# A shared feed-forward stage and an expert stage joined into one program: weights split early, experts unrolled, two scatters in flight

## The reference

```python
x = x + attention0(layernorm(x), ctx, ctx)
# mixture of experts, E = 8, top 2, I = 352, shared part SI = 704
f = layernorm(x); scores = softmax(f @ gate_w.T)
w = scores * one_hot(top_k(scores, 2)).sum(1)
g, u = split(einsum('nh,eih->nei', f, experts_gate_up))
out = einsum('neh,ne->nh', einsum('nei,ehi->neh', silu(g) * u, experts_down), w)
shared = silu(f @ shared_gate_w.T) * (f @ shared_up_w.T) @ shared_down_w.T
x = x + out + sigmoid(f @ shared_expert_gate_w.T) * shared
x = x + attention1(layernorm(x), ctx, ctx)
x = x + low_rank_experts(layernorm(x))    # gates by the first token
```

## Time and profile before

| what | us |
|---|---|
| median of 3 runs | 612.63 (612.49 to 616.44) |
| the profiled execution | 613.12 |
| span of its trace, first to last instruction | 611.3 |
| mean granted TensorE clock | 0.927 |
| PE / DVE / POOL / ACT busy | 489.3 / 296.7 / 213.2 / 194.1 |
| shared stage's last matmul ends | 252.7 |
| expert matmuls begin / end | 256.0 / 416.7 |
| attention 1 begins | 460.5 |

### The profile page before, as it was taken

One profiled execution on the slowest core, in us unless ns is written; L12 is line 12 of the kernel. 1 busy time (PEld: TensorE's weight loads), 2 busy tenths in 40 slices (PEclk: granted clock), 3 DMA queues, 4 the chain that ended last, 5 costly groups with the idle time before them and its releaser, 6 DMA issues. The chain is left out here.

```text
span 611.3 us, 9853 instructions
## 1 busy us (share of the span) xinstructions
PE 489.3 (80%) x3126; PEld 393.3 (64%) x3127; DVE 296.7 (49%) x674; ACT 194.1 (32%) x426; POOL 213.2 (35%) x259
## 2 busy tenths in 40 slices
PE   4799996599999998748999999992004798998587
PEld 3567663476877775647999999991003566666465
DVE  4678785631541211224455554441006478977574
ACT  2455543474500210012333333330002355453044
POOL 3110320343403773342793222233224436420055
PEclk9999999699999998879999999997556899999799
DMA  8993000200001325259412222211107200000003
GB/s 306 395 387 99 1 1 0 80 0 2 1 0 38 109 92 122 71 201 358 165 34 72 80 71 69 69 55 41 43 34 254 90 1 1 1 2 2 0 19 120
DMA packets 37747, 53.30 MB, mean 87 GB/s; under 512 B 8945, under 2 KB 31986, under 8 KB 37458
## 3 DMA queue, kind: packets, MB, share of 16 engines
q1 hardware_dynamic: 28482, 23.19, 12.9%
q0 software_dynamic: 6032, 22.55, 10.2%
q10 hardware_dynamic: 3200, 7.14, 3.2%
HBM read 35.78 MB, written 17.10 MB: 86 GB/s over the span
## 5 line engine op out<-in xcount | busy, mean ns | idle before, releaser
L112 POOL TENSOR_TENSOR rstd<-var,mhalf 128x2 f32<-128x2 f32 x32 | 22.6, 706 | 137.2 <-DVE var L105 137.2
L1174 PE MATMUL banks<-w_hi,xgT_hi 128*128 x156 | 57.1, 367 | 11.1 <-POOL w_lo L1143 7.7
L1252 ACT ACTIVATE hg<-banks 128x352 f32<-128x352 f32 x39 | 18.1, 465 | 123.2 <-PE banks L1178 123.2
L1310 DVE TENSOR_TENSOR hgT_lo<-banks,hgT_hi 128x256 fp32r<-128x256 f32 x78 | 24.1, 351 | 67.4 <-ACT hgT_hi L1260 67.4
L411 DVE TENSOR_REDUCE mx<-banks 128x16 f32<-128x1024 f32 x32 | 39.1, 1223 | 32.2 <-PE banks L272 31.8
L1175 PE MATMUL banks<-w_lo,xgT_hi 128*128 x156 | 51.5, 331 | 0.0
L272 PE MATMUL banks<-kvb,qT 64*128 64x256 f32 x256 | 36.3, 401 | 17.8 <-ACT qT L358 6.6
L944 PE MATMUL banks<-sdn,big 128*128 128x256 f32 x192 | 49.0, 403 | 0.0
L148 PE MATMUL banks<-ctxT,wk 128*128 128x128 f32 x16 | 4.1, 439 | 51.3 <-PEq L1112 43.8
L944 PEld LDWEIGHTS banks<-sdn,big 128*128 128x128 f32 x192 | 35.1, 195 | 13.2 <-issue 9.3
L123 ACT ACTIVATE xn<-x,shift,rstd 128x256 f32<-128x256 f32 (+1 forms) x64 | 34.7, 593 | 27.5 <-POOL shift L114 26.3
(11 more groups left out here) (223 smaller groups left out, 1162.2 us busy)
## 6 DMA issues: line engine op xcount, KB each, us to landing
w_hi<-in_egu POOLq DMA_DIRECT2D x2, 2816.0 KB, 21.3
expert_rows_in<-zeros SPq DMA_DIRECT2D x1, 5304.0 KB, 42.2
xn<-expert_rows_in SPq DMA_DIRECT2D x39, 128.0 KB, 2.1
w_lo<-in_egu ACTq DMA_DIRECT2D x3, 1408.0 KB, 9.9
y_all<-choices_out SPq DMA_DIRECT2D x16, 256.0 KB, 5.9
out_x<-fo SPq DMA_DIRECT2D x8, 256.0 KB, 2.1
x<-in_x ACTq DMA_DIRECT2D x2, 768.0 KB, 11.3
d_hi<-in_edown POOLq DMA_DIRECT2D x1, 1536.0 KB, 7.8
```

The source lines that it names most:

```text
L112: nc.gpsimd.tensor_tensor(m["rstd"][:, b, :], m["var"][:, b, :], m["mhalf"][:, :], ALU.pow).then_inc(self.rstd_ready, 1)
L1174: nc.tensor.matmul(psum[bank + c][:, 0:I], xgT_hi[:, c, k, :], w_hi[:, k, at], start=(k == 0), stop=False)
L1310: ins = nc.vector.tensor_tensor(hgT_lo[rows, c, ks, :], h[rows, ks, :], hgT_hi[rows, c, ks, :].bitcast(F32), ALU.subtract)
```

## The change

Names: `wd` is one memory [128, 8 x 2944] that holds per expert w_lo (1408), d_hi (768) and d_lo (768). It is laid over memory that the shared stage frees step by step, so each load and subtraction waits for the event that frees its part. The barrier and the block at line 1112 go; all engines run on from the shared stage's code. Row buffers grow from two to four (`NX`, both halves of `xn`). The experts' part is unrolled over 39 blocks on all engines. The order within a block of slots is as before. The two attentions share one set of semaphores with counts that go on (`Event`); nothing else changes there.

```diff
-        xg = mem["xn"][:, 0, :, :]
+        xg = mem["xn"][:, :, :, :].rearrange("p b t n -> p (b t) n")
+        NX = 4
+        def load_w(act, e, end, here):                 # KD = 2 DMAs
+        def load_d(engine, e, end, lo, here):          # KI = 3 DMAs, runs of 1 KB
+        def make_w_lo(eng, e):                         # one subtraction, 128 x 1408
+        def make_d_lo(eng, e):                         # two, 128 x 512 and 96 x 256
+        def fetch(sp, b):
+            wait(sp, bt_ready, b - NX + 1)
 # SP
                 sp.wait_ge(scattered, 16 * 2 * NT)
-                fetch(sp, 0, 0)
-                fetch(sp, 0, 1)
-                fetch_first_chunk(sp)
+                for b in range(NX):
+                    fetch(sp, b)
                 sp.dma_start(slot_w[:, 0:w_first, :], ...)
                 sp.dma_start(slot_w[:, w_first:NB, :], ...)
+                for b in range(NX, NB):
+                    fetch(sp, b)
 # POOL, behind the 32nd scatter of rows
+                    if j == 1:
+                        pool.wait_ge(u_ready, 4 * KS)
+                        pool.wait_ge(h2_done, 2 * KS)
+                        load_d(pool, 0, 5, 0, d_hi_in[0])
                     pool.wait_ge(scattered, 16 * NT * (j + 1))
+                pool.wait_ge(w_hi_in, 16 * KD)
+                pool.wait_ge(lo_made, 2)
+                for e in range(2, E):
+                    if e == 2 or W_GROUP[e] > W_GROUP[e - 1]:
+                        pool.wait_ge(w_in[W_GROUP[e]], ...)
+                    make_w_lo(nc.gpsimd, e)
+                    if e == 2:
+                        pool.wait_ge(d_in, 16 * KI)
+                        pool.wait_ge(d_hi_in[0], 16 * KI)
+                        pool.wait_ge(d_lo_made, 1)
+                        make_d_lo(nc.gpsimd, 1)
+                        pool.wait_ge(d_ready, 16)
+                        load_d(pool, 5, E, 0, d_hi_in[1])
+                    if e == 5:
+                        pool.wait_ge(d_hi_in[1], 16 * KI)
+                    make_d_lo(nc.gpsimd, e)
+                for b in range(NB):
+                    pool.wait_ge(by_done, b + 1)
+                    wait(pool, by_out[b % 2], 16 * (b // 2))
+                    pool.indirect_dma_start(...).then_inc(by_out[b % 2], 16)
 # ACT, behind its last silu of the shared stage
-                copy_rows(0, 0)
+                act.wait_ge(u_ready, 4 * KS)
+                load_w(act, 0, 1, w_in[0])
+                load_d(act, 0, 4, 1, d_in)
+                load_w(act, 1, 2, w_in[1])
+                load_w(act, 2, 4, w_in[2])
+                act.wait_ge(h2_done, 2 * KS)
+                act.wait_ge(ranked, 1)
+                load_w(act, 4, 5, w_in[3])
+                load_d(act, 4, 5, 1, w_in[3])
+                act.wait_ge(scattered, 16 * 2 * NT)
+                load_w(act, 5, 6, w_in[4])
+                load_d(act, 5, 6, 1, w_in[4])
+                copy_rows(0)
+                act.wait_ge(d_ready, 16)
+                load_w(act, 6, E, w_in[5])
+                load_d(act, 6, E, 1, w_in[5])
 # PE, behind down(3)
+                pe.wait_ge(w_hi_in, 16 * KD)
+                pe.wait_ge(h2_done, 2 * KS)
+                NR = 4                     # experts' numbers per register load
+                load_experts(0)
+                for b in range(NB):
+                    e = expert(b)
+                    half(b, 0, 1, bg_ready, bsilu, e)
+                    if b == 0:
+                        pe.wait_ge(sh_added, NT)
+                    if b > 0:
+                        transpose_h(b - 1)
+                    if b + 1 < NB:
+                        transpose_rows(b + 1)
+                    half(b, 1, 3, bu_ready, bh_done, e)
+                    if b > 0:
+                        expert_down(b - 1, previous)
+                    if b % NR == NR - 2 and b + 2 < NB:
+                        load_experts(b + 2)
 # DVE, behind add(2)
-                split_rows(0, 0)
+                dve.wait_ge(w_hi_in, 16 * KD)
+                for e in range(2):
+                    dve.wait_ge(w_in[e], 16 * KD)
+                    make_w_lo(v, e)
+                split_rows(0)
                 add(3)
                 dve.wait_ge(sh_added, NT)
+                dve.wait_ge(d_in, 16 * KI)
+                dve.wait_ge(d_hi_in[0], 16 * KI)
+                make_d_lo(v, 0)
                 dve.wait_ge(slot_w_in, 16)
+                # then per block: split_h, split_rows, hidden_rows, take_y
```

More of the change, by code:

```diff
@@ L42, with __init__ @@
 SCALE = DH ** -0.5
+class Event:
+    def __init__(self, sem):
+        self.sem, self.before = sem, 0
 def wait(engine, sem, value):
@@ L506, in _ @@
                 other_work("gpsimd", 2 * u + 1)
+    for n, total in ATTENTION_EVENTS.items():
+        events[n].before += total
 def top_two(nc, dve, sem, base, p, rev, work, shape, low):
@@ L745, in xattn_ffn_kernel @@
         w_first = 6
[L747 to L753 removed]
+        until_shared_ends.close()
+        here = lambda name, shape, dt=F32: stage_memory(until_experts_end, name, shape, dt)
+        hh, hg = here("hh", [P, 2, I]), here("hg", [P, 2, I])
@@ new lines, in yy, with d_part @@
+        def yy(b):
+            n = b % NY
+            if n < NY - 8:
+                return y_rows[:, n, :]
+            half = mem["qT" if n < NY - 4 else "xT"][:, (n - NY) // 2 % 2, :, :].rearrange("p k n -> p (k n)")
+            return half[:, (n - NY) % 2 * D:((n - NY) % 2 + 1) * D]
+        def d_part(e, lo):
+            at = e * EALL + EW + lo * ED
+            return wd[:, at:at + ED].rearrange("p (k n) -> p k n", k=KI)
+        def load_w(act, e, end, here):
+            for k in range(KD):
+                act.dma_start(of_expert[:, e:end, k * 2 * I:(k + 1) * 2 * I].bitcast(F32),
+                              egu_in[k * P:(k + 1) * P, e * 2 * I:end * 2 * I].rearrange("p (e n) -> p e n", e=end - e)).then_inc(here, 16)
@@ new lines, in half @@
+                def half(b, w, bank, done, taken, e):
+                    wait(pe, bT_done, b + 1)
+                    wait(pe, taken, b - 1)
+                    pe.wait_ge(lo_made, e + 1)
+                    c, to = b % 2, psum[bank + b % 2][:, 0:I]
+                    for k in range(KD):
+                        hi, lo = w_hi[:, k, ds(e * (2 * I) + w * I, I)], wd[:, ds(e * EALL + (k * 2 * I + w * I), I)]
+                        nc.tensor.matmul(to, xgT_hi[:, c, k, :], hi, start=(k == 0), stop=False)
+                        nc.tensor.matmul(to, xgT_hi[:, c, k, :], lo, start=False, stop=False)
+                    wait(pe, bL_done, b + 1)
+                    for k in range(KD):
+                        last = nc.tensor.matmul(to, xgT_lo[:, c, k, :], w_hi[:, k, ds(e * (2 * I) + w * I, I)],
+                                                start=False, stop=(k == KD - 1))
+                    last.then_inc(done, 1)
```

427 lines of the change are left out of this document (150 added, 277 removed).

## The result

The changed kernel takes 591.59 us (median of 4 runs, 590.34 to 595.98), the old one 613.77 (median of 4). The ratio is 0.9646, 95% interval 0.9584 to 0.9708. So the kernel became faster by 22 us; the forecast was 565, a gain of 48, with a range that ended at 579.

The account below looks back on a forecast made before the run. PE bounded only the expert stage's middle; load waits bounded its start, POOL's late, one-at-a-time scatters its end. Gains 35.4 + 3.3 + 1.3 + 14.1, less cost 6.3, net 47.8 off 613.12, half a microsecond off for the median: 565 us, range 554 to 579.

Parts of the forecast that it names:

- (c): Expert stage's start: earlier weight loads remove the stall for w_lo(1) and the slow blocks behind it; gain 14.1 us.
- (f): Unrolled expert blocks: PE between -4 and +6 us in all, taken as 0; ACT, DVE and SP not late.
- (a): Expert stage's end: two scatters in flight take POOL off the path; gain 35.4 us.
- R2: Rival on the expert stage's scatters: they don't overlap and the pitch stays 3.24 us; 576 us, chance 0.08.
- (b): Expert stage's start: no barrier, w_lo of experts 0 and 1 before down(3); gains 3.3 us idle and 1.3 us clock.
- (d): Before the first expert block: loads delay the scatter of rows and the first fetch; cost 6.3 us.
- The 0.9 for a longer low clock: At down(3): PE's longer gap makes its low clock level last 2 us longer; loss 0.9 us.
- (e): slot_w's two loads on SP's queue, beside the weight loads: from no cost to 5 us late, taken as 0.
- R4: Rival on PE's sequencer in the unrolled blocks: extra address operations make the kernel slower; 631 us, chance 0.02.
- the 2 us left for PE's clock: After the expert stage: 2 us either way for PE's clock at the next stage's start.
- R1: Rival before the first expert block: loads go before rows, delaying scatter and fetch by 14 us; 578 us, chance 0.17.
- R3: Rival for the expert stage: (d) costs nothing and the pitch falls to 3.60 us; 555 us, chance 0.17.

Follow-up runs that it names:

- e3b_psum: Changed kernel with the block numbers copied to PSUM and `spread` kept there, so `spread` and `dest` each have one SBUF operand; 571.7 us, ratio 0.9303.
- e1: Changed kernel with DVE's `spread` and `dest` instructions moved ahead of d_lo(0); 571.76 us, ratio 0.9319.
- e6: Changed kernel with POOL waiting for its own last subtraction of each expert before the next; 571.33 us.
- e7: Program of e3b_psum with one scatter in flight, as in the old kernel, instead of two; 591.04 us.
- e11: Program of e3b_psum with only ACT's loads for experts 4 and 5 issued behind its first copy of rows; 576.91 us, ratio 0.9345.
- e2: Changed kernel with POOL waiting for `dest` ahead of its subtraction for expert 5, DVE's program unchanged; 576.38 us.
- e4: Changed kernel with `spread` and `dest` at block 5 instead of block 2; 583.52 us.
- e10: Old kernel with `spread` and `dest` moved from behind block 2's work to behind block 7's; 616.75 us, the old kernel beside it 617.68.
- e5b: Program of e3b_psum with weight loads not yet needed held behind the first row fetch or the high down parts; 577.05 us, ratio 0.9405.

## Why the prediction was wrong

The stage ended 24.4 us later than forecast, and the terms are these.

- **The step that failed is an overlap, in (c) and (f)**: "So all 14.1 us go" together with "ACT, DVE, SP lose their loops; they aren't late". The old stall did go: in e3b_psum outputs 0 to 6 take 21.8 us, against 36.29 in the earlier trace rows. But (c) moved POOL's row of subtractions itself, to 262:294, and never asked which instruction of DVE then stood beside it. Outputs 1 to 3 took 28.04 us (271.84 to 299.88) where two blocks take 7.3: 20.7 us lost, nearly all of it the 19.8 of `spread` and the 1 us more of `dest`. PE's granted clock was 0.63 in 272:292, where PE had gone idle, and 0.50 in 292:296 behind it. Removing the hold in three ways (e1, e3b, e6) gives 571.8, 571.7 and 571.3 us, 20 below the kernel after and 6 to 7 above the forecast. In e3b_psum's profile the next stage starts at 416.24, 3.5 us behind the forecast 412.7, and what follows takes 155.9 us instead of 150.8; the old kernel beside it took 2.6 us more than the median that the forecast started from. None of my rivals contained the hold.
- **(a)**: the tail is 10.5 us (437.11 - 426.64) instead of the forecast 8.3. Start and landing came as said (1.27 against 1.24, and 2.4); drain and entry take 6.8 instead of 4.6. They take 6.8 in e7 too, with one scatter in flight, so this belongs to the new program and not to the second scatter; what it consists of is open. What the step credits to two scatters in flight, 35.4 us, was too much: with one in flight e7's tail is 34.2 us (439.01 - 404.81), with two in e3b_psum 10.5, a difference of 23.7; the other 9.5 of the old 43.7 went in e7 already, whose queue starts 27 us earlier. R2 also took its pitch of 3.24 from the last row alone: the 38 intervals from 321.83 to 453.45 are 3.46 us each.
- **(b)**: right. No PE wait for w_lo(0), expert matmuls follow down(3) directly, and the granted clock is 1.00 in their first 4 us (260:264) instead of 0.59.
- **(d)**: right in kind, somewhat small. The scatter landed in 5.5 us (I had 4.4) and the fetch in 6.4 (5.5). PE waited 10.4 us instead of 8. The 0.9 for a longer low clock did not come: down(3) took 13.43 us against 13.34. So block 0 started at 260.34 instead of 259. Behind it PE stood 1.6 us more for ACT, which issues five loads from 260.45 on; (f) had counted ACT as never late.
- **(e)**: 0, as taken, but near: slot_w landed at 259.0 here, at 270.0 in e1's profile and at 276.8 in e11's, where DVE came to use it at 277.84.
- **(f), pitch**: (420.81 - 299.88) / 33 = 3.66 us a block, against 3.70; unrolling cost PE nothing, R4 falls. (Its price of 0.12 us for an operation is in no run; the earlier trace rows have 0.046.)
- **What follows the stage**: 151.2 us here, against 150.8, as said. But the 2 us left for PE's clock were too few in general: e3b_psum's profile has 155.9 us, with a granted clock of 0.56 in the first 33 us after the stage, where the kernels before and after have 0.79 and 0.78. Why PE's clock rose later there is open.

Together: 20.7 (hold) + 1.3 (block 0) + 1.6 (ACT) - 1.4 (pitch, 36 blocks by 0.04) + 2.2 (drain) = 24.4. POOL held until 262.56, the first scatter at 294.06 (261 and 293 forecast) and DVE as the scatters' releaser came as forecast; R1, R2 and R3 did not happen.

What stays open: why POOL's back-to-back row lets the held instruction in at one end of an instruction and not at another. In the kernel after it was passed over eleven times and let in with two POOL instructions left in the row; in e2, e4 and for `dest` in e10 also with two left, in e6 with one. That could be the moment at which POOL has no further instruction issued, but this is not shown: `spread` in e10 got in at 304.6, in mid-row, and no run separates this further. The hold was tested with one DVE operation only, a scalar_tensor_tensor of 128x39, beside POOL's f32 subtractions.

## What to carry to other kernels

When work moves in time, list every instruction that will run beside it, on both engines, and not only who waits for whom by semaphores: an unchanged 0.2 us instruction became 20 us long without any semaphore between it and its blocker. A VectorE instruction with two SBUF operands is a risk beside a row of GpSimd tensor instructions; give it a PSUM operand, an early or late place, or give GpSimd one wait on itself per round. A stall that is free, as in e10, can be the whole cost once another queue no longer hides it. In a profile, the sign is a window in which an engine is fully busy with one or two instructions.

## What the runs showed of the hardware

- A 128x39 instruction on DVE with both operands in SBUF took 0.19 to 0.20 us with POOL idle, and 19.77, 14.99, 9.54, 4.92, 4.03 and 1.15 us beside POOL's subtractions, ending in each case 0.05 to 0.06 us behind the end of a POOL instruction. The section of the Trainium skill named above calls the shared ports an exclusive lock and says, of DVE's two-port modes, that whoever issues first has them for the whole instruction and the other is fully blocked. The trace shows more: the hold went on over eleven ends of POOL instructions, as long as the next ones followed without a pause.
- The other direction was not seen: POOL's 128x512 subtraction took 1.25 us in the held stretch of the kernel after and 1.27 to 1.31 outside it.
- A 128 KB fetch and a row scatter beside queued loads landed in 6.4 and 5.5 us, and in e5b, with the weight loads held back, in 2.1 and 2.5.
